# Attention and expert kernel: relative terms in one pass, query rows by DMA, blockwise division, new order on each engine

## The reference

```
# layer 0: windowed attention with relative positions, then an MLP
xn   = layer_norm(x) * w + b, padded to 28 x 28 and cut into windows of 14 x 14
attn = (q * 0.25) k^T + rel_h[y_q - y_k] . q + rel_w[x_q - x_k] . q
x    = x + softmax(attn) v @ proj + b ;  x = x + gelu(layer_norm(x) @ fc1) @ fc2
# layer 1: causal attention over the 256 tokens of an image, then experts
t = t + softmax(causal(q k^T / 16)) v @ lin
t = t + sum over the top 2 of 8 experts of gate_e * (gelu(ln(t) @ w1_e + b1_e) @ w2_e + b2_e)
```

## Time and profile before

| | |
|---|---|
| median of 3 runs | 904.73 us (902.12 to 910.28) |
| span of the profiled execution | 902.0 us; its own time isn't shown apart from the span |
| busy: PE, PEld | 774.4 us (86%), 677.2 us (75%) |
| busy: DVE, ACT, POOL | 456.8, 334.5, 134.9 us |
| chain that ended last | PE 71%, DVE 16%, DMA 4%, issue 3%, SPq 3% |
| relative terms (L1767) | 512 matmul rows, busy 80.1 us |
| division of A (L1231) | 24 reciprocals, busy 42.1 us |
| transfers | 72.16 MB, mean 80 GB/s |

### The profile page before, as it was taken

One profiled execution on the slowest core, in us unless ns is written; L12 is line 12 of the kernel. 1 busy time (PEld: TensorE's weight loads), 2 busy tenths in 40 slices (PEclk: granted clock), 3 DMA queues, 4 the chain that ended last, 5 costly groups with the idle time before them and its releaser, 6 DMA issues.

```text
span 902.0 us, 15569 instructions
## 1 busy us (share of the span) xinstructions
PE 774.4 (86%) x5670; PEld 677.2 (75%) x5670; DVE 456.8 (51%) x1113; ACT 334.5 (37%) x724; POOL 134.9 (15%) x241
## 2 busy tenths in 40 slices
PE   5359989989988998998899899886868999999990
PEld 3347867877877876887688688675767999999980
DVE  3072465675765766356576766655354422222223
ACT  5103234343442452334144245233336344444430
POOL 5000000010201111020112102102111321121220
PEclk9965789998997997589799799869989899999996
DMA  6890762102102112010211120173822111111116
GB/s 220 216 225 10 169 159 80 38 18 76 55 23 70 46 37 64 18 54 19 71 46 36 39 77 21 39 200 109 255 69 80 58 46 41 41 44 42 42 31 218
DMA packets 62047, 72.16 MB, mean 80 GB/s; under 512 B 6370, under 2 KB 52286, under 8 KB 61846
## 3 DMA queue, kind: packets, MB, share of 16 engines
q1 hardware_dynamic: 58566, 64.17, 26.2%
q0 software_dynamic: 3408, 7.02, 2.3%
HBM read 27.26 MB, written 23.17 MB: 56 GB/s over the span
## 4 chain that ended last, share of the span: by engine, by line
PE 71%; DVE 16%; DMA 4%; issue 3%; SPq 3%; POOL 2%; ACT 1%; DVEq 0%; ACTq 0%; POOLq 0%
PE ps L2068 8%; PE ps L1725 7%; PE ps L1726 6%; PE ps L1767 6%; PE ps L2051 6%; PE ps L2052 6%; PE ps L1910 3%; PE ps L1811 3%; PE ps L1883 3%; DVE max_rows_a L1211 3%; PE ps L1849 3%; PE ps L1934 3%; PE ps L1835 3%; DVE den L1231 3%; PE ps L1730 2%
## 5 line engine op out<-in xcount | busy, mean ns | idle before, releaser
L2051 PE MATMUL ps<-rows_t,w_tile 97*128 97x128 f32 x468 | 91.1, 276 | 2.1 <-DVE rows_t L1440 2.1
L2052 PE MATMUL ps<-rows_t,w_tile 96*128 96x128 f32 x468 | 90.5, 274 | 0.0
L2068 PE MATMUL ps<-w_exp,hid_t 128*128 x468 | 84.9, 332 | 2.2 <-DVE y_out L1448 1.4
L1273 DVE TENSOR_REDUCE max_b<-ps 128x3 f32<-128x384 f32 x96 | 48.9, 551 | 68.7 <-PE ps L1951 67.4
L1767 PE MATMUL ps<-s_q,rel_w 128*128 128x96 f32 x512 | 80.1, 318 | 2.2 <-DMA s_q<-staged_a 1.2
L1431 DVE COPY w_tile<-w_exp 96x768 f32 x39 | 21.7, 556 | 114.6 <-PE ps L2052 112.8
L2068 PEld LDWEIGHTS ps<-w_exp,hid_t 128*128 128x128 f32 x468 | 76.9, 194 | 3.5 <-issue 3.4
L1767 PEld LDWEIGHTS ps<-s_q,rel_w 128*128 128x128 f32 x512 | 73.7, 207 | 3.2 <-DMA s_q<-staged_a 1.8
L838 ACT ACTIVATE probs_a<-ps 98x392 f32<-98x392 f32 x96 | 47.8, 498 | 75.4 <-PE ps L1838 73.0
L2051 PEld LDWEIGHTS ps<-rows_t,w_tile 97*128 97x128 f32 x468 | 72.9, 191 | 3.0 <-DVE rows_t L1440 3.0
L2052 PEld LDWEIGHTS ps<-rows_t,w_tile 96*128 96x128 f32 x468 | 71.0, 191 | 0.0
(11 more groups left out here) (223 smaller groups left out, 1675.0 us busy)
## 6 DMA issues: line engine op xcount, KB each, us to landing
xs_dram<-blank SPq DMA_DIRECT2D x32, 388.0 KB, 8.7
w_exp<-in_e_w SPq DMA_DIRECT2D x16, 576.0 KB
ks_a<-staged_a SPq DMA_DIRECT2D x32, 192.0 KB, 3.2
qs_b<-staged_b SPq DMA_DIRECT2D x32, 192.0 KB, 3.0
ks_b<-staged_b SPq DMA_DIRECT2D x32, 192.0 KB, 3.2
tile_x<-xs_dram SPq DMA_DIRECT2D x39, 97.0 KB, 1.9
w_exp<-y_dram SPq DMA_DIRECT2D x8, 384.0 KB, 6.4
rel_w<-in_rel_tables SPq DMA_DIRECT2D x1, 1792.0 KB, 10.3
```

The source lines that it names most:

```text
L1273: ins = dv.tensor_reduce(max_b3[:, h, :], BANK_C[:, h % 3, 0:384].rearrange("p (a k) -> p a k", a=3), AX.X, ALU.max, negate=True).then_inc ...
L2051: pe.matmul(dst, w1_tile[t % 2][:, 0, cols], rows_t[t % 2][:, 0, :], start=True, stop=False)
L2052: ins = pe.matmul(dst, w1_tile[t % 2][0:DC, 1, cols], rows_t[t % 2][0:DC, 1, :], start=False, stop=True)
L2068: ins = pe.matmul(TILE_Y[:, 0:D], hid_t[t % 2][:, f, :], w_exp[:, bass.ds(e, 1), 2 * MLP + f * D:2 * MLP + (f + 1) * D].rearrange("p e d - ...
```

## The change

It computes the same. Relative terms: `queries_a` rounds to the high part and DVE makes the low part (`low_queries_a`); `s_q` holds both, twice, and the tables hold high and low parts too, so that one fp32r pass sums the four products. The result has 64 partitions for both slots and no queries in it. The tables come from eight smaller transfers into a blanked tile, in pieces of 32 numbers, in place of one of 1792 KB. The queries themselves now go to `qs_a` by four transfers, after POOL has put them in windows order (`query_windows`). The marks of the key windows, formerly loaded into `s_q`, are written once into `qs_a` by POOL, ahead of its first norm. Division of A is that of B. Counts of the routing are bf16. Norms are cut into `sums_for_*` and `norm_*`. Values of A write PSUM in image order, in three pieces in place of two. The order on every engine is new.

```diff
             def queries_in_a(i):
-                sp.wait_ge(qh_a, i + 1)
...
-                for e in range(2):
-                    sp.dma_start(s_q[SLOT * e:SLOT * e + HD, :, :], staged_a[:, e, :]).then_inc(q_in_a, 16)
+                for low, ready in enumerate((qh_a, ql_a)):
+                    sp.wait_ge(ready, i + 1)
+                    for e in range(2):
+                        for part in range(2):
+                            first = SLOT * e + 2 * HD * part + HD * low
+                            sp.dma_start(s_q[first:first + HD, :, :].bitcast(F32), staged_a[:, 2 * low + e, :]
+                                         ).then_inc(s_in_a, 16)
+            def query_rows_in_a(i):
+                if i:
+                    sp.wait_ge(av_a, GROUPS * i)
+                for low, first in enumerate((HIGH, LOW)):
+                    sp.wait_ge(qw_a, 2 * i + low + 1)
+                    for twice in range(2):
+                        sp.dma_start(qs_a[first + twice:first + 2 * HD:2, :, :].bitcast(F32),
+                                     staged_a[:, 8 + 2 * low:10 + 2 * low, :]).then_inc(q_in_a, 16)
...
             def positions(bank, j, table, toks):
-                dst = bank[:, j * 96:(j + 1) * 96].rearrange("p (g x) -> p g x", g=PAIRS)
+                dst = bank[0:SLOT, j * 96:(j + 1) * 96].rearrange("p (g x) -> p g x", g=PAIRS)
...
             def max_a(p):
                     if p == 0:
                         pe.wait_ge(q_done, i + 1)
+                        pe.wait_ge(q_in_a, 64 * (i + 1))
                         pe.wait_ge(k_in_a, 64 * (i + 1))
...
             def normalise_a(g):
-                    dv.stream_shuffle(den[:, :], src, [HD] * 32).then_inc(dn_a, 1)
-                    dv.reciprocal(den[:, :], den[:, :]).then_inc(rc_a, 1)
+                    dv.transpose(o_cols[:, :], BANK_Z[:, 0:TOK]).then_inc(dn_a, 1)
+                    after(dv.reciprocal(sums_a[:, :], blocks[:, :, HD]))
+                    after(dv.tensor_tensor(blocks[:, :, 0:HD + 1], blocks[:, :, 0:HD + 1],
...
+                    dv.transpose(o_a[:, g, :], o_cols[:, :]).then_inc(ot_a, 1)
```

More of the change, by code:

```diff
@@ L529, in last @@
                 tile_rows(12)
+                for i in c:
+                    store_t2(i)
+                    clear_row_b(i)
                 tile_rows(13)
@@ L584, in _ @@
             gp.memset(ones[:, :], 1.0).then_inc(zeros_set, 1)
+            gp.wait_ge(marks_in, MARKS_IN)
+            hold(gp)
+            for dst, src in zip(win_order(qs_a[0:SLOT, :, :]),
+                                window_pieces(yx(marks.unsqueeze(1).to_broadcast([SLOT, HEADS, TOK])))):
+                ins = gp.tensor_copy(dst, src)
+            ins.then_inc(marked, 1)
             def rstds(k):
@@ L955, in step @@
                     exp_b(4)(i)
+                for i in b:
+                    channels_m(i)
+                for i in c:
                     exp_b(5)(i)
                 for i in b:
-                    channels_m(i)
+                    gelu(0)(i)
                 for i in a:
@@ L1453, in step @@
                 for i in c:
+                    sums_for_b(i)
+                for i in b:
+                    reduce_a(0)(i)
+                for i in d:
+                    tables(i)
+                for i in c:
                     norm_b(i)
+                for i in b:
+                    reduce_a(1)(i)
                 for i in d:
@@ L1517, in step @@
                 for i in a:
+                    rel_columns(3)(i)
                     split_odd(i)
+                for i in c:
+                    out_b(i)
+                    sums_for_g(i)
+                for i in a:
                     split_even(i)
                 for i in c:
-                    out_b(i)
                     norm_g(i)
@@ L2017, in count @@
                 counts = routing(i)[1]
-                pe.matmul(counts, before[:, :], both[:, :, :].rearrange("p t e -> p (t e)"), start=True, stop=False)
+                pe.matmul(counts, before16[:, :], both[:, :, :].rearrange("p t e -> p (t e)"), start=True, stop=False)
                 pe.matmul(counts[:, NE:2 * NE], ones[:, :], both[:, 0, :], start=False, stop=False)
@@ L2154, in step @@
                 for i in c:
-                    attend_b(1)(i)
                     attend_b(2)(i)
                     attend_b(3)(i)
+                for i in b:
+                    transpose_m(i)
                 for i in a:
                     rel_columns(2)(i)
+                    rel_columns(3)(i)
                 for i in c:
@@ L2162, in step @@
                     attend_b(5)(i)
-                for i in a:
-                    rel_columns(3)(i)
+                for i in b:
+                    fc1(0)(i)
                 for i in c:
```

562 lines of the change are left out of this document (322 added, 240 removed).

## The result

The changed kernel takes 971.1 us (median of four runs, 963.6 to 976.6) against 907.5 for the kernel before beside it: a ratio of 1.081, 95% interval 1.071 to 1.092. (The two medians divide to 1.070; some executions fall into a slower state, as one of the kernel before with 923.4 us beside three of 902.1 to 910.3, and the ratio is taken over those outside it.) The forecast was 929, with a range from 888 to 950: the direction was right, the size was not. The profiled execution has a span of 961.7 us, 59.7 more than before.

The account below looks back on a forecast made before the run. TensorE bounds the tile loop; steps follow hand-overs between engines and transfers. Start 18, step 1 0, steps 2 to 7 5, step 8 3, last stage -1: +25 on 902.0, plus 2.7, gives 929 us; range 888 to 950.

Parts of the forecast that it names:

- relative terms: Attention A's rows and columns matmuls: 0.08 us each, 2.6 us an image, 6.1 less than now.
- The short value matmuls: Values of attention A: 16 short half-passes of a group become 32, +0.32 us a group, 1.0 an image.
- Leg 3: Steps 2 to 7, max_b(0) to the first relative matmul: 13.8 us before, +0.2 (values +1.0, v_a_out -0.8).
- The start: Up to the first maximum: fills ahead of query rows and keys move it from 54.9 to 73 us, +18.
- leg 2: Steps 2 to 7, last reduce's end to max_b(0): 8.6 us before, +2.2, TensorE idle waiting for the late queries.
- leg 6: Steps 2 to 7, last values to next first maximum: 14.6 us before, +2.2, rows and keys queued behind store_t2.
- step 8: Expert loads between row, keys and queries cost +8 us, legs 1, 4 and moved fc1 give 5 back: +3.
- Leg 4: Steps 2 to 7, first relative matmul to attend_b(0): 7.5 us before, 4.8 after, -2.7 from shorter relative terms and division.
- rival (c): More low clock: 5 us idle ahead of each step's first phase, two more stretches like 339 to 424 give 955; 0.13.
- leg 1: Steps 2 to 7, first maximum to the end of the last reduce: 16.5 us before, set by the reduces, -1.4.
- The last stage: Behind step 8: expert 6 ahead of the keys +4 us, tiles starting among the maxima -5: -1.
- Rival (a): Faster: waits of legs 2 and 6 don't come, a step takes 62.2 us and the kernel 864; chance 0.20.

Follow-up runs that it names:

- the run with the fills behind: Changed kernel with the 16 fills of steps 0 and 1 moved behind query rows and keys in SyncE's queue: 952.1 us, ratio 1.048.
- both moves: Changed kernel with B's queries and keys ahead of A's row of maxima, and A's query rows and keys right behind B's row: 830.1 us, ratio 0.917.
- with filler: Changed kernel with 14 matmuls of 128 columns added ahead of the wait of max_b(0), no wait removed: 934.1 us, ratio 1.028.
- the run with A's transfers early: Changed kernel with A's query rows and keys right behind B's row of maxima, ahead of fills, store and next image: 904.3 us, ratio 0.999.
- experiment on the load of the tokens: Changed kernel with both moves, expert 6 ahead of B's last-stage queries, token load moved from tile 21 to behind tile 12, last image's store behind tile 9: 824.3 us.
- the kernel before with its queries late: Kernel before with B's queries moved behind A's row of maxima and B's keys in SyncE's queue: 948.7 us, ratio 1.047.
- both kernels with a filler: Changed kernel with 14 matmuls ahead of max_b(0)'s wait, 934.1 us; kernel before with B's queries late and 7 matmuls there, 914.4 us.
- The kernel with B's transfers early: Changed kernel with B's queries and keys ahead of A's row of maxima, low parts among DVE's reduces: 899.3 us, ratio 0.988.
- the kernel with the relative terms three times: Kernel with both moves, every matmul of the relative terms issued three times into the same place: 853.8 us, ratio 0.947.

## Why the prediction was right or wrong

The relative terms were priced well: 0.08 us was taken for each, 0.059 for rows and 0.086 for columns measured, 2.3 us an image for the 2.6 of the sum. Half of the 0.08, the lower bound for half the weight columns, was too low for both. But it halved the wrong row: beside the half-passes of the kernel before, which have the same 96 moving columns and 128 weight columns (0.112 and 0.159), the new ones with their 64 take 0.53 and 0.54 of the time. The short value matmuls were held too dear: the two short pieces of a group take 0.41 us at the high clock (340.14 to 340.55) for 0.32 before, 0.3 us an image and not 1.0. Leg 3 came to its 14.0 at the high clock even so, so some other part of it was held too cheap.

The start was right: fills ahead of query rows and keys, 73 forecast, 74.96 measured, and 53.8 in the run with the fills behind. Two smaller errors met in it: the fills were issued from 38.92 and not from 41, and from there to the first maximum it took 36 us and not 32. The small pieces of the new tables cost nothing that can be seen; their issues in the changed kernel (count, KB each, median us to landing):

```profile
staged_a<-in_rel_tables SPq DMA_DIRECT2D x8, 56.0 KB, 2.7
```

They are issued by 13.0 us, and their first reader, a cast on ACT at 22.58, doesn't wait for them.

The legs were right, with TensorE at its high clock (1.00 in legs 2 to 5 of both moves), all but leg 4. The forecast beside the runs (step 4; us):

| Leg | before | forecast | after | with filler | both moves |
|---|---|---|---|---|---|
| 1 | 16.5 | 15.1 | 15.5 | 15.7 | 14.5 |
| 2 | 8.6 | 10.8 | 10.5 | 10.6 | 6.2 |
| 3 | 13.8 | 14.0 | 19.9 | 14.0 | 14.0 |
| 4 | 7.5 | 4.8 | 2.9 | 3.0 | 2.8 |
| 5 | 10.9 | 11.1 | 11.2 | 10.9 | 11.2 |
| 6 | 14.6 | 16.8 | 17.2 | 17.2 | 10.6 |

The waits came where they were put, for the reason given, and nearly as long as worked out: leg 2 10.8 and 10.5, leg 6 16.8 and 17.2. With the filler the whole step is 71.5 us, the forecast 72.7. That the time of the filler run, 934, lies so near the forecast of 929 is in part luck: its steps 2 to 7 take 428.6 us, 24 under the forecast 452.6 (the kernel before had its cold step in there), and step 8 with all behind it takes 357.2, 24 above the forecast 333.2. Leg 4 was held 1.9 too long: the transposes of B's maxima now run ahead of the relative rows, so the row is under way earlier than I had it.

**The step that failed** is the price of leg 3, "+0.2", which took the high clock for granted behind an idle that leg 2 had just added. The prediction had the price in the earlier trace rows (the cold step, 85.00 us at 0.76 for 72.00 at 0.93, 13 more) and wrote that an idle of 5 us now stands ahead of each step's first phase, but it did so only in rival (c), as two more accidental stretches, with 0.13. It set the idle ahead of max_a(0) beside the clock, and not the one ahead of max_b(0). Measured, they differ: behind the idle of leg 6 the clock is low too (0.72 in leg 1), but there DVE's reduces set the pace, and it costs 2 to 3 us (leg 1 of 15.5 to 16.4 in steps 3 to 7, against 13.5 at a clock of 1.00 in the run with A's transfers early). Behind the idle of leg 2 TensorE sets the pace (busy for 13.24 of 13.24 us at 0.50 in step 4) and leg 3 takes 19.9 to 22.0 for 14.0, 6 to 8 us a step, 40 in the six. The table above has only 20.7 us for the six steps, since the kernel before has a cold step among its own and the new order, at the high clock, is the shorter one. The profile of before shows what was needed. Its legs 2 and 3 in windows:

```profile
283.70:292.28 8.58, 8.52 (x44) 7.20 (x45) 1.86 (x10) 2.26 (x7) 0.00 (x0) 0.80 0.33 93
292.28:306.10 13.82, 13.39 (x178) 11.46 (x178) 10.90 (x25) 7.46 (x24) 0.00 (x0) 1.00 0.07 19
```

TensorE is busy for 13.4 of the 13.8 us of leg 3 at a clock of 1.00: nothing there can hide a clock of 0.50. And the 0.80 of leg 2 is a fall of the same kind: behind a pause of 1.23 us, in which the transposes for row_a wait for the last reduce, the clock is at 0.50 from 284.5 to 287.7. Every step from 2 to 7 has that pause and that fall; in most it is over before max_b(0). I had put a price on leg 3's instructions and none on the clock at which they run.

Step 8, "+3": the two experts' loads brought TensorE a wait of 13.4 us, leg 2 took 19.9 us where before it was 7.3, 12.6 more, where I had counted 8. Of the 5 given back only 1.6 came. The mechanism was right, the size was not. The step that failed stands in here too: TensorE is at 0.50 from 629.5 to 664.5, so for 19 us behind max_b(0), and in the kernel before for 7 us behind it. No run parts the one from the other in this step.

The last stage, "-1": the wait for the keys grew by 5.1 us (4 were forecast), and the 5 us that the tiles were to give back did not come. They start later and not sooner behind max_b(0) (first result at 25.2, before at 22.7 us), and the token load, which I had counted as out of their way, now stands in the middle of their loop, where TensorE is without a gap and every delay counts: tiles 19 to 21 take 12.4 us for 9.7. The experiment on the load of the tokens shows that it costs some 3 us at either place among the tiles. The 10.5 us of this stretch are 6.4 up to max_b(0), 5.1 of them the wait and the rest ahead of it, where the clock is at 0.50 from 695 on (in the kernel before only for 4 us, from 646 to 650); 2.5 to the first result; and 1.6 in the tiles and the end. What delays the first result was not traced.

Rival (a), the waits that don't come, was a statement about the kernel's order and not about the change's parts: with the two moves the kernel does what (a) described, at 830 and not 864. Its profiled execution is 31 us under the span that goes with (a): 19 are the start, which (a) left at +18 and which the move of A's transfers took away (53.8 for 72.9); 22 are the six steps (61.2 us on average for 64.9 with the cold one); step 1 gives 4, and from step 8 on 15 are lost.

## What to carry to other kernels

Where a change adds an idle of TensorE, price it twice, as it was paid here: once as the wait (4.1 to 4.6 us a step), and again as the work behind it at the low clock (0.50; 6 to 8 us a step), if TensorE sets the pace there and not another engine. Look in the profile of before for short pauses with a fall behind them: here the clock was at 0.50 behind one of 1.23 us. A transfer's place in its issuing queue can cost more than its own time: query rows and keys that could have gone out 20 us earlier cost 6 us a step because they stood behind a store that waits for a result late in the step. Where a wait can't be moved, a few matmuls into a bank that is about to be overwritten may win back the second price (here it was 37 us of 971, with work added, and 34 of 949 in the kernel before with its queries late).

## What the runs showed of the hardware

An idle of 2.0 us (the kernel before with queries late, step 4) was followed by a leg at a granted clock of 0.54 with TensorE busy throughout; one of 4.1 us by 13.2 us at 0.50. In both kernels with a filler 0.2 to 1.6 us of idle were left ahead of max_b(0), and the clock stayed at 1.00 through leg 3 in all twelve steps.

The length of the idle alone doesn't tell whether the clock falls, nor for how long: 1.60 us ahead of max_b(0) in step 7 of the changed kernel with the filler left it at 1.00. In the kernel before, every step from 2 to 7 has a pause of 1.22 or 1.23 us ahead of row_a, and the clock falls to 0.50 behind each (in step 4 from 284.5 to 287.7). In steps 2, 3, 4 and 7 it is back after some 3 us, in step 6 after 7, and in step 5 only after 34, with TensorE busy nearly all the while:

```profile
355.50:358.00 2.50, 2.41 (x9) 2.18 (x10) 1.90 (x11) 0.36 (x1) 0.00 (x0) 0.62 0.01 3
358.00:361.00 3.00, 3.00 (x9) 2.25 (x9) 0.00 (x0) 0.48 (x1) 0.00 (x0) 0.50 0.78 223
...
378.00:391.50 13.50, 13.50 (x108) 10.39 (x108) 5.86 (x13) 3.02 (x10) 0.00 (x0) 0.55 0.02 6
```

That is where the 85.5 us of step 5 come from: its leg 2 is 4.3 us longer than in step 4 and its leg 3 9.3. The kernel with B's transfers early has such a step as well (leg 3 of 24.3 in step 5), and the kernel with the relative terms three times one (20.1 in step 7); the kernel with both moves has none in steps 3 to 7. What sets the length of a low stretch was not settled.

One-pass fp32r matmuls of 64 weight columns and 96 moving ones run at 0.059 us each when the moving operand is read in one piece, and at 0.086 when it is read with a stride. The half-passes of fp32 before it, with 128 weight columns and the same moving ones, ran at 0.112 and 0.159.
